# A two-layer graph and mixture-of-experts kernel: where layer one's bias is added, and the form of the slot loop

## The reference

```python
x = x + gnn(layernorm(x), adj, ...)           # quantized support, adj (2048x2048) @ support
xf = layernorm(x)
probs = softmax(xf @ Wr + br);  topk_w, topk_idx = top_k(probs, 2)   # weights then sum to 1
h = einsum('nc,ech->neh', xf, W1) + b1        # layer one with its bias
h = layernorm_affine(h, g1, be1)              # eps 1e-5
h = gelu(h, approximate=False)
y = einsum('neh,eho->neo', h, W2) + b2        # only the two chosen experts count
x = x + sum(topk_w * y[chosen])
```

## Time and profile before

| what | value |
|---|---|
| median of 3 runs | 520.58 us (520.26 to 522.81) |
| profiled execution | 522.36 us |
| its span, first to last instruction | 520.6 us |
| mean granted PE clock | 0.969 |
| busy PE / DVE / ACT / POOL | 475.4 / 352.4 / 289.5 / 234.2 us |
| HBM read, written | 68.05 MB, 19.40 MB |
| instructions in the trace | 10405 |

### The profile page before, as it was taken

The page is one execution under the profiler, slowest core; times in us unless marked ns, Lnnn a source line. Parts: engine busy times, 40 slices in busy tenths (PEclk is TensorE's granted clock), DMA queues, the critical chain, the costliest instruction groups (busy, mean ns, idle before and its releaser), DMA issues. The chain is left out here.

```text
span 520.6 us, 10405 instructions
## 1 busy us (share of the span) xinstructions
PE 475.4 (91%) x2328; PEld 390.6 (75%) x2329; DVE 352.4 (68%) x732; ACT 289.5 (56%) x484; POOL 234.2 (45%) x269
## 2 busy tenths in 40 slices
PE   1789999999999997489999999999999999999981
PEld 1478888878888887368888888888877878888760
DVE  5898856746786867858667667677778666776420
ACT  1665633634444434428667766768867757764440
POOL 4355401513454536244364555465553544555422
PEclk9999999999999997689999999999999999999986
DMA  8522222864886521056875785875797896644433
GB/s 298 241 82 76 67 81 82 271 224 170 306 295 231 179 102 63 23 151 223 238 205 122 224 244 127 198 217 108 225 272 223 254 279 164 152 79 74 73 57 40
DMA packets 31625, 87.75 MB, mean 169 GB/s; under 512 B 6032, under 2 KB 6176, under 8 KB 31088
## 3 DMA queue, kind: packets, MB, share of 16 engines
q1 hardware_dynamic: 17504, 56.53, 33.1%
q0 software_dynamic: 9488, 22.55, 21.4%
q10 hardware_dynamic: 4608, 8.39, 4.3%
HBM read 68.05 MB, written 19.40 MB: 168 GB/s over the span
## 5 line engine op out<-in xcount | busy, mean ns | idle before, releaser
L622 POOL DMA_INDIRECT xg<-xn_rows,tok_i x41 | 48.2, 1176 | 97.8 <-ACT gate L843 82.5
L864 ACT ACTIVATE g_sb<-ps,be_sb,g_sb 128x128 f32<-128x128 f32 x160 | 60.2, 457 | 56.7 <-PE ps L1492 56.7
L647 POOL DMA_INDIRECT out<-y_sb,scat_i x37 | 65.7, 1776 | 21.7 <-DMA out<-y_sb,scat_i 11.4
L1227 DVE TENSOR_TENSOR w_lo<-w_raw,w_hi x58 | 68.4, 1221 | 9.2 <-issue 8.4
L1234 DVE TENSOR_SCALAR h_hat<-ps,h_mv,h_rs 128x512 f32<-128x512 f32 x40 | 32.4, 809 | 49.0 <-issue 32.0
L702 ACT ACTIVATE adj_hi<-adj_raw,small 128x1024 fp32r<-128x1024 f32 x32 | 36.8, 1150 | 49.1 <-PE ps L1334 43.2
L965 DVE SCALAR_TENSOR_TENSOR adj_lo<-adj_raw,small,adj_hi 128x1024 fp32r<-128x1024 f32 x32 | 40.7, 1273 | 26.5 <-ACT adj_hi L702 26.4
L836 ACT ACTIVATE w_hi<-w_raw x29 | 54.8, 1914 | 5.7 <-DMA w_raw<-in_w 5.1
L578 POOL TENSOR_SCALAR rstd<-mv 128x1 f32<-128x1 f32 x15 | 14.6, 973 | 80.7 <-DVE mv L1011 80.7
L1334 PE MATMUL ps<-sup,adj_lo 128*128 128x512 f32 x192 | 49.2, 398 | 0.0
L1334 PE MATMUL ps<-sup,adj_hi 128*128 128x512 f32 x192 | 49.0, 397 | 0.0
(11 more groups left out here) (181 smaller groups left out, 952.5 us busy)
## 6 DMA issues: line engine op xcount, KB each, us to landing
w_raw<-in_w SPq DMA_DIRECT2D x64, 512.0 KB
adj_raw<-in_adj_steps SPq DMA_DIRECT2D x32, 512.0 KB, 3.5
out<-x_sb ACTq DMA_DIRECT2D x16, 256.0 KB, 2.8
xn_rows<-xn ACTq DMA_DIRECT2D x16, 256.0 KB, 2.4
x_sb<-in_x SPq DMA_DIRECT2D x3, 1024.0 KB, 12.6
gw_raw<-in_gnn_w SPq DMA_DIRECT2D x1, 1024.0 KB, 5.0
x_sb<-in_x SPq DMA_DIRECT2D x2, 512.0 KB, 6.9
xg<-xn_rows,tok_i POOLq DMA_INDIRECT x41
```

The costliest lines, as they stand in the source:

```text
L622: return pool.indirect_dma_start(to[:, s % 2, :], None, xn_rows, bass.IndirectOffsetOnAxis(ap=tok_i[:, s:s + 1], axis=0)).then_inc(landed[ ...
L647: pool.indirect_dma_start(out, bass.IndirectOffsetOnAxis(ap=at, axis=0), y_sb[:, par, :], None, compute_op=ALU.add).then_inc(scattered[par ...
L864: ins = act.activation(g_sb[:, par, c * P:(c + 1) * P], ht_ps(par)[:, c * P:(c + 1) * P], ACT.Gelu, scale=g1_sb[:, bass.ds(e_s * C + c, 1) ...
L1227: ins = dve.tensor_tensor(w_lo[:, n, at], w_raw[:, n, :, :].rearrange("p a n -> p (a n)")[:, at], w_hi[:, n, at].bitcast(F32), ALU.subtract)
```

## The change

1. **Layer one's bias.** SP loads the fp32 row of the expert to all 128 partitions (`b1_rows`, 256 KB) in place of the two rows of 4 KB. PE's bias matmul of layer one goes. DVE adds the row to the hidden values in PSUM and writes them to SBUF (`h_sb`); statistics and `h_hat` read them there. b1 is no longer split, stored and zeroed ahead; b2 still is.
2. **Epsilon.** DVE's epsilon (L1219) goes; POOL adds it from a column of constants ahead of its power, as an instruction of its own that the power waits for.
3. **The loop.** The first six pairs run without a test; the other 16 turns stand in four blocks of four, each block behind a test of its own, each turn in it too. On POOL the same, unrolled. With 18 pairs used, three blocks run whole and one is left out by its test.
4. **Tile 14's router** moves ahead of tile 15's transposes on PE; `gate_values(3)` moves behind `choose(4)` on DVE.
5. **Batch 4's rows** (four hits) go from ACT to POOL (two) and DVE (two, `last_rows`), as comparisons.

The diff, cut to its core:

```diff
+SURE = E // 2 - 2
+BLOCKS = (SLOTS // 2 - 2 - SURE) // 4
+assert SURE + BLOCKS * 4 == SLOTS // 2 - 2
...
-        bias_row = [place(f"bias_row{n}", [P, 4 * D], F32R) for n in (1, 2)]
+        b1_rows = place("b1_rows", [P, 4 * D], F32)
+        bias_row = place("bias_row", [P, 4 * D], F32R)
+        h_sb = place("h_sb", [P, 2, D], F32)
...
             def load_bias(n, e, ring):
-                sp.dma_start(bias_row[n][0:2, ring].bitcast(F32), bias_dram[n, e]).then_inc(raw_in[n], 16)
+                if n:
+                    sp.dma_start(bias_row[0:2, ring].bitcast(F32), bias_dram[e]).then_inc(raw_in[n], 16)
+                else:
+                    row = e if not isinstance(e, int) else slice(e, e + 1)
+                    sp.dma_start(b1_rows[:, ring], b1[row, :].broadcast_to([P, D])).then_inc(raw_in[n], 16)
...
-                for n in range(2):
-                    for h, half in enumerate((bias_hi, bias_lo)):
-                        sp.dma_start(bias_dram[n, :, h, :], half[32 * n:32 * n + E, :].bitcast(F32)).then_inc(bias_out, 16)
+                for h, half in enumerate((bias_hi, bias_lo)):
+                    sp.dma_start(bias_dram[:, h, :], half[0:E, :].bitcast(F32)).then_inc(bias_out, 16)
...
-            for base, b in ((0, b1), (32, b2)):
-                pool.dma_start(b_raw[base:base + E, :], b).then_inc(bias_in, 16)
+            pool.dma_start(b_raw[0:E, :], b2).then_inc(bias_in, 16)
...
-                if last == 2 * BATCHES[b][1]:
+                if last == (2 if b == 4 else 2 * BATCHES[b][1]):
                     ins.then_inc(rows_hit, 1)
...
             dense_gates(4)
+            row_hits(4, 0, 2)
...
             def slot_rstd(s, par):
 
                 pool.wait_ge(h_var, s + 1)
+                pool.tensor_tensor(h_rs[:, par, 2:3], h_mv[:, par, 1:2], const("eps"), ALU.add).then_inc(h_eps, 1)
+                pool.wait_ge(h_eps, s + 1)
                 pool.tensor_tensor(h_rs[:, par, 0:1], h_rs[:, par, 2:3], neg_half, ALU.pow).then_inc(h_rstd, 1)
...
-            for j in range(1, SLOTS // 2 - 1):
-                with pool.If(rest > j - 1):
-                    earlier, word = load_begins(pool, j - 1), load_begins(pool, j)
-                    for s in (2 * j, 2 * j + 1):
-                        slot_rstd(s + 1, (s + 1) % 2)
-                        fetch(s)
-                        give(s - 1, (word & 1) if s % 2 else (earlier >> 1))
+            def pool_pair(j):
+                earlier, word = load_begins(pool, j - 1), load_begins(pool, j)
+                for s in (2 * j, 2 * j + 1):
+                    slot_rstd(s + 1, (s + 1) % 2)
+                    fetch(s)
+                    give(s - 1, (word & 1) if s % 2 else (earlier >> 1))
+
+            for j in range(1, SURE + 1):
+                pool_pair(j)
+            for b in range(BLOCKS):
+                with pool.If(rest > SURE + b * 4):
+                    for j in range(SURE + b * 4 + 1, SURE + b * 4 + 5):
+                        with pool.If(rest > j - 1):
+                            pool_pair(j)
...
-            t0, n = BATCHES[4]
-            row_set = hit_sets[0][1]
-            act.wait_ge(placed_ok, 5)
-            for j in range(2 * n):
-                ins = act.activation(row_set[:, j, :], const("minus_row"), ACT.Square, scale=-1.0,
-                                     bias=where_f[:, 0, 0, j % 2, j // 2:j // 2 + 1])
-            ins.then_inc(rows_off, 1)
-            act.wait_ge(rows_off, 1)
-            rows = row_set[:, 0:2 * n, :].rearrange("p a b -> p (a b)")
-            act.activation(rows, rows.bitcast(F32), ACT.Relu, scale=-1.0, bias=const("ones")[:, 0:1]).then_inc(rows_hit, 1)
...
-            with act.Fori(1, SLOTS // 2 - 1) as j:
-                with act.If(j < rest + 1):
-                    word = load_plan(act, j)
-                    for par in range(2):
-                        slot(j * 2 + par, par, word, j * 16 + 16 * par)
+            def act_pair(j):
+                word = load_plan(act, j)
+                for par in range(2):
+                    slot(j * 2 + par, par, word, j * 16 + 16 * par)
+
+            with act.Fori(1, SURE + 1) as j:
+                act_pair(j)
+            with act.Fori(0, BLOCKS) as b:
+                with act.If(b * 4 < rest - SURE):
+                    with act.Fori(0, 4) as i:
+                        with act.If(b * 4 + i < rest - SURE):
+                            act_pair(b * 4 + i + (SURE + 1))
...
+            def last_rows():
+
+                for j in range(2, 4):
+                    ins = dve.tensor_scalar(hit_sets[0][1][:, j, :], const("minus_row"),
+                                            where_f[:, 0, 0, j % 2, j // 2:j // 2 + 1], None, ALU.is_equal)
+                ins.then_inc(last_rows_hit, 1)
...
             norm_last(T - 1)
-            gate_values(3)
             add_br(T - 2)
             val_hits(2, 3, 6)
             val_hits(3, 0, 6)
             add_br(T - 1)
             pick(4)
             choose(4)
+            gate_values(3)
             gate_values(4)
             find(4)
             val_hits(4, 0, 4)
+            last_rows()
...
-            def slot_stats(s, par):
+            def slot_stats(s, par, e):
                 dve.wait_ge(mm1, s + 1)
-                link(dve.bn_stats(h_stats[:, par, :], h_ps(par)))
+                link(dve.tensor_tensor(h_sb[:, par, :], h_ps(par), b1_rows[:, bass.ds((e & 3) * D, D)], ALU.add))
+                link(dve.bn_stats(h_stats[:, par, :], h_sb[:, par, :]))
                 dve.sem_inc(dve_turn, 1)
-                link(dve.bn_aggr(h_mv[:, par, :], h_stats[:, par, :]))
-                dve.tensor_scalar(h_rs[:, par, 2:3], h_mv[:, par, 1:2], LN_EPS, None, ALU.add).then_inc(h_var, 1)
+                dve.bn_aggr(h_mv[:, par, :], h_stats[:, par, :]).then_inc(h_var, 1)
...
-                dve.tensor_scalar(h_hat[:, par, :], h_ps(par), h_mv[:, par, 0:1], h_rs[:, par, 0:1], ALU.subtract, ALU.mult
+                dve.tensor_scalar(h_hat[:, par, :], h_sb[:, par, :], h_mv[:, par, 0:1], h_rs[:, par, 0:1], ALU.subtract, ALU.mult
...
             finish_t(T - 2)
             rank(3)
+            router(T - 2)
             finish_t(T - 1)
-            router(T - 2)
             router(T - 1)
...
-                pe.matmul(dst, two_rows[:, :], bias_row[n][:, bass.ds((e & 3) * D, D)], start=True, stop=False)
+                if n:
+                    pe.matmul(dst, two_rows[:, :], bias_row[:, bass.ds((e & 3) * D, D)], start=True, stop=False)
                 for c in range(C):
-                    pe.matmul(dst, act_hi[:, par, c * P:(c + 1) * P], w_hi[:, n, at[c]], start=False, stop=False)
+                    pe.matmul(dst, act_hi[:, par, c * P:(c + 1) * P], w_hi[:, n, at[c]], start=not n and c == 0, stop=False)
```

## The result

The changed kernel took **522.92 us** (median of 8, 521.68 to 523.70) beside 521.24 us before (median of 8): a ratio of 1.0031, interval 1.0017 to 1.0045. So the change is worth nothing, or costs some 0.3%. The forecast was 517.6 us, 3 us faster; 522.92 lies inside its range of 512.0 to 523.5, but on the wrong side of before. The profiled execution took 522.95 us.

What follows compares the result with a forecast made beforehand. PE bound the slot loop, VectorE where new experts start. Loop -2.5, exit -1.0, head 0 and transfers +0.5 made -3.0 us: 519.4 us for the profiled execution, 517.6 us as median; range 512.0 to 523.5 us.

Steps and rivals of the forecast that it cites:

- PE's part: Slot loop: dropping layer one's bias matmul saves 0.25 us a slot, 6.87 to 6.62 us, 9.3 us over slots 2 to 38.
- VectorE's part: Per slot: sum adds 0.73 us, h_hat from SBUF saves 0.15, epsilon's removal 0.2; net +0.38 us, ends +0.14 and +0.49.
- the rule of the Trainium skill: h_hat on VectorE: single-source SBUF-to-SBUF operations run two elements a cycle; by it h_hat would give 0.24 us more per slot.
- VectorE's busy time: Sign that the forecast is right: VectorE's busy time goes up by some 15 us.
- the walk: Slots 2 to 38 stepped through by queue rules: PE waits 9.8 us for h_hat, loop net -2.6 us, taken as -2.5.
- PE's waits for h_hat: Sign that the forecast is right: they grow from 3.8 to 10 us or so, mostly between 355 and 410 us.
- The idle before the last h_hat: Sign of a right forecast at the loop's exit: VectorE's idle there comes to near 3 us.
- The loop's form: Loop's end: empty turns fall from four to one block test, saving PE 1.0 us, lower end 1.7 us.
- the rival on the slower side: Pair edges in the last twelve pairs: the nested loop delays VectorE's queue before h_hat; +3.5 us, 524.1 us, chance 0.18.
- Transfers: Layer one's bias as 256 KB loads, 4.0 MB in all, ahead of the weights: +0.5 us, ends 0 and 3 us.
- Head: Before the loop: `tok_i` comes 1.0 us earlier, but the second h_hat stays where it was; 0, from -1 to +1 us.
- the rule on GpSimd held by VectorE: VectorE instructions with two SBUF inputs hold up GpSimd ones reading SBUF; epsilon add 0.35 us in the loop, upper end 1.16.

Runs made afterwards that it cites:

- e_small: Changed kernel with layer one's bias rows loaded to 2 partitions (4 KB), the others zeros, so that bias is mostly left out: 519.86 us, ratio 0.9959 to before.
- after: The changed kernel itself, in its first measurement and profile: 522.92 us, ratio 1.0031 to before.
- e_loop_pieces: Kernel before with the loop in blocks of four and the head's 2048-wide `w_lo` subtractions cut in four: 521.04 us, ratio 0.9987.
- after2: The changed kernel, unchanged, measured and profiled a second time: 522.26 us, ratio 0.9996 to before.
- e_bias: Kernel before with only layer one's bias sum on VectorE and the epsilon on GpSimd, old loop and head: 523.25 us, ratio 1.0040.
- e_bias2: Kernel before with the bias and epsilon parts alone, measured a second time: 525.55 us, ratio 1.0061.
- e_eps: Changed kernel with the epsilon back on VectorE, behind `bn_aggr`: 523.55 us, ratio 1.0037 to before.
- e_pieces: Changed kernel with each of the head's 2048-wide `w_lo` subtractions on VectorE cut into four of 512 columns: 519.24 us, ratio 0.9959 to before.

## Why the prediction was wrong

**PE's part** held. The slot is 6.62 us where nothing is late: slot 30 to 37 took 46.33 us in seven slots.

**VectorE's part** was mis-sized to its favour. The sum took 0.68 us, as its row said. h_hat took 0.55 us at the mean, between the two values that were weighed (0.66 and 0.42). That is a half-way case for the rule of the Trainium skill (VectorE: DVE Perf Modes, What auto-detection actually checks): 0.55 us against 0.81 us from PSUM is faster, but not the 0.42 us of the row that fits it. Why it took 0.55 us is open. VectorE's busy time rose by 8.8 us in the loop, not 15. Against an even 6.62 us a slot, e_small, without the transfers, lost 8.3 us from slot 1 to 37 where the walk had 9.8; the 0.7 us that it had between slots 31 and 34 were not there. PE's waits for h_hat from 225 us on came to 10.4 us, and that they are near the 10 us forecast is luck: 2.1 us stand at the start, 3.1 in the spell and 2.1 at the exit, and only 2.7 between 355 and 410 us, where most were to be. The idle before the last h_hat came to 2.85 us, near the 3 us said:

```profile
502.45 0.55 DVE L1258 TENSOR_SCALAR h_hat<-h_sb,h_mv,h_rs 128x512 f32<-128x512 f32 x1 [2.85 <-issue]
```

**The loop's form** held in its mechanism and was sized too small: -1.0 us was forecast, the exit gave 1.5 us in after and 1.9 us alone. The nest at each block edge costs nothing that can be seen, so the rival on the slower side fell: the time moved its way, but by 1.7 us or less, not 3.5, and not for its reason.

**Transfers: +0.5 us was the term that failed in the loop.** Slots 1 to 37 gained 3.8 us without the extra bytes, more than the 2.5 forecast. With them the gain was 2.2 us in one profile and -0.3 us in the other. The cost is 1.6 and 4.1 us, the second beyond the end of 3 us that was given. The forecast went by who waits for the weights (ScalarE, 5.1 us before, 6.8 after), and the way was another: a late scatter, then `y_sb`, then the scatter at which GpSimd stands, then the power behind it. The prediction named the scatter queued behind the power, not the power queued behind the scatter.

**Head: 0 was the term that failed most.** It came to +3.3 and +3.7 us. The step that VectorE gains 1.0 us up to `tok_i` and the second h_hat comes out where it was took everything behind `tok_i` to keep its order. But the new head also took VectorE's wait for PE away, and a `w_lo` of 2.3 us that had started 0.12 us behind a gather's issue now started 0.33 us ahead of it. The prediction used the rule on GpSimd held by VectorE for the epsilon and the power alone. For the gather's issue the trace of before had the sign of it too, in a gather that took 1.94 us. The rule that it drew from the Trainium skill (SBUF - State Buffer, Who interferes with whom) was borne out by the epsilon: 0.54 us beside the pieces against 2.14 us. And in after the head's wait of 2.11 us, in place of 1.34, was followed by another 3.5 us at half clock, which no term held.

**The sum, and what is left open.** The forecast's loop and exit together, -3.5 us, would have been -5.3 (3.8 + 1.5) without the transfers; with 3.5 us at the start and 2 to 4 for the transfers the change ends where it began. Why the spell's size changes between executions is open, and a form that brings the bias in without 256 KB per expert was not tried. That the changed kernel's median lay inside the range of 512.0 to 523.5 us says nothing for the forecast's reasons.

## What to carry to other kernels

When a step is made earlier, lay the other engines' queues beside its new time: a GpSimd instruction that just missed a long VectorE operation with two SBUF inputs may now meet it. Cutting such an operation in four costs 0.2 us and gave back 3.7 us here by the medians; in e_loop_pieces, where no gather that PE waited for stood beside it, it gave nothing. And a load that "fits in the mean rate" is judged where the rate is highest, by who stands in a queue behind the transfer that it delays.

## What the runs showed of the hardware

The issue of an indirect gather on GpSimd took 2.79 us when it started 0.33 us behind a VectorE subtraction with both inputs in SBUF (2.29 us long), and 0.98 us when it started 0.12 us ahead of it; beside the same work in pieces of 512 columns it took 1.20 us. So it isn't arithmetic on GpSimd alone that waits.

TensorE's granted clock fell to half behind the wait of 2.1 us for the first h_hat in five profiles out of five (after, after2, e_bias, e_bias2, e_small); in after PE had worked at full clock for some 4 us between the last half-clock stretch and that wait. Behind a wait of 2.05 us (e_eps) and those of 1.50 us and less at the same place it did not. It cost 1.3 us each time, for slot 0 to 1 took 5.04 to 5.08 us in place of 3.7 to 3.8. The length of a wait alone does not decide it: at the exit a wait of 2.13 us was followed by half clock in after2 and not in after, and one of 1.76 us was in before; at slot 28 waits of 3.08 and 3.30 us were (after, e_pieces) and one of 2.90 us was not (e_eps). Executions of one kernel (e_bias) differ by up to 18 us in the time at half clock, estimated from the mean granted clock, and by 7 us in all.
